# Graph attention on one core: the first four score steps moved in between the value tiles, and the first output tiles' wait lowered by one read

## The reference

```
q = (x @ wq + bq).reshape(N, H, Dh) * Dh ** (-0.5)      # H = 4, Dh = 128
k = (x @ wk + bk).reshape(N, H, Dh)
v = (x @ wv + bv).reshape(N, H, Dh)
scores = jnp.einsum('ehd,ehd->eh', q[src], k[dst])       # one for each edge
... softmax over the edges of each src
out = jax.ops.segment_sum(attn[:, :, None] * v[dst], src, num_segments=N)
return out.reshape(N, D) @ wo + bo
```

## Time and profile before

| | us |
|---|---|
| median of 3 runs | 2468.97 |
| the 3 runs | 2466.75 to 2469.61 |
| the profiled execution, device time | 2466.02 |
| its span in the profile | 2464.0 |
| mean granted TensorE clock | 0.991 |

### The profile page before, as it was taken

The page is one execution under the profiler, slowest core; times in us unless marked ns, Lnnn a source line. Parts: engine busy times, 40 slices in busy tenths (PEclk is TensorE's granted clock), DMA queues, the critical chain, the costliest instruction groups (busy, mean ns, idle before and its releaser), DMA issues. The chain is left out here.

```text
span 2464.0 us, 28010 instructions
## 1 busy us (share of the span) xinstructions
PE 2383.1 (97%) x9352; PEld 1404.5 (57%) x9352; DVE 1428.1 (58%) x2941; ACT 963.0 (39%) x1663; POOL 898.5 (36%) x1246
## 2 busy tenths in 40 slices
PE   8999999999999999999999999999999999998998
PEld 4665655555676646577556567655567664533343
DVE  7896760523775753677564477655377655633345
ACT  5885642221664211566111266321166522211221
POOL 2005202030654430365341165352056443425564
PEclk9999999999999999999999999999999999999999
DMA  5401101320666110366210166410056611679737
GB/s 165 136 18 33 42 13 51 105 88 18 154 154 184 69 59 18 93 156 162 63 42 22 50 163 155 120 44 22 18 133 160 171 42 51 207 236 330 220 91 233
DMA packets 138271, 264.22 MB, mean 107 GB/s; under 512 B 52990, under 2 KB 54766, under 8 KB 135788
## 3 DMA queue, kind: packets, MB, share of 16 engines
q1 hardware_dynamic: 93118, 159.79, 22.3%
q0 software_dynamic: 43664, 100.31, 15.1%
q10 hardware_dynamic: 1346, 2.33, 0.3%
HBM read 212.80 MB, written 31.93 MB: 99 GB/s over the span
## 5 line engine op out<-in xcount | busy, mean ns | idle before, releaser
L114 POOL DMA_DIRECT2D cols<-w x720 | 352.8, 498 | 591.9 <-DVE w L810 576.2
L693 PE MATMUL psum<-cols,rows 128*128 128x256 f32 (+1 forms) x1600 | 370.0, 379 | 7.1 <-DMA cols<-w 7.1
L679 PE MATMUL psum<-g_k_cols,g_q_cols 128*125 128x512 f32 (+1 forms) x960 | 361.4, 513 | 2.5 <-DVE g_row_max L796 2.5
L873 ACT ACTIVATE g_prob<-g_prob,g_row_max 125x1250 f32<-125x1250 f32 x160 | 214.0, 1338 | 306.1 <-DVE g_row_max L796 304.4
L693 PEld LDWEIGHTS psum<-cols,rows 128*128 128x128 f32 (+1 forms) x1600 | 303.4, 190 | 47.0 <-DMA cols<-w 8.5
L796 DVE CUSTOM_DVE_ANT_0 g_prob<-psum,ln_count 125x1250 f32<-125x1250 f32 x160 | 233.6, 1460 | 141.0 <-PE psum L679 141.0
L679 PEld LDWEIGHTS psum<-g_k_cols,g_q_cols 128*125 128x125 f32 x960 | 179.4, 187 | 172.7 <-issue 161.1
L810 DVE STREAM_TRANSPOSE w<-g_prob 128x1280 f32<-128x1280 f32 x160 | 241.2, 1507 | 11.2 <-ACT g_prob L879 11.2
L879 ACT ACTIVATE g_prob<-g_prob,g_row_max 125x1250 f32<-125x1250 f32 x160 | 214.0, 1338 | 58.3 <-DVE g_row_max L786 58.3
L2813 PE MATMUL psum<-m_ew,m_x_cols 128*64 128x256 f32 (+1 forms) x576 | 152.4, 495 | 7.2 <-DMA cols<-in_L_ffn_expert_w,m_weights_of 6.3
L749 PE MATMUL psum<-w,g_k_cols 128*125 128x512 f32 x320 | 150.6, 616 | 0.0
(11 more groups left out here) (393 smaller groups left out, 3967.5 us busy)
## 6 DMA issues: line engine op xcount, KB each, us to landing
cols<-w POOLq DMA_DIRECT2D x720, 80.0 KB, 3.3
cols<-w SPq DMA_DIRECT2D x560, 80.0 KB
m_eb<-in_L_ffn_expert_b SPq DMA_DIRECT2D x54, 192.0 KB
w<-in_L_gnn_m_w SPq DMA_DIRECT2D x8, 1024.0 KB
slot_rows<-p_kf SPq DMA_DIRECT2D x1, 7128.0 KB, 32.7
rows<-slot_rows SPq DMA_DIRECT2D x54, 132.0 KB, 2.9
m_ew<-in_L_ffn_expert_w SPq DMA_DIRECT2D x4, 1536.0 KB, 12.1
slot_outputs<-slot_rows SPq DMA_DIRECT2D x1, 5000.0 KB
```

Source lines behind the costliest of these rows:

```text
L114: return eng.dma_start(out, in_, allow_slow_non_contiguous=True)
L679: ins = pe.matmul(psum[0:P, at:at + width], q_cols[:, h, t * P:(t + 1) * P], k_cols[:, h, start:start + width], start=True, stop=True)
L693: ins = pe.matmul(c.bank(6 + g % 2, 256).rearrange("p (u a i) -> p u a i", u=2, a=SIDE), rows[0:r, j, h * 128:(h + 1) * 128], turned_keys[ ...
L873: s.activation(prob[0:P, u, 0:N], prob[0:P, u, 0:N], ACT.Exp, bias=row_max[:, u, 0:1], scale=-1.0, accum_out=row_max[:, u, 2:3]).then_inc( ...
```

## The change

All of it is in the graph network's layers and holds for each of the four.

- PE's order at a layer's start: values 0 to 3, `scores(0)`, values 4 and 5, `scores(1)`, values 6 and 7, `scores(2)`, value 8, `scores(3)`, value 9, then `scores(4)` and on as before.
- DVE's order follows it: the bias additions, score reads, sums and transposes of the first steps are interleaved in the same way. `turn_squares(2)` still waits for all ten value tiles and now stands ahead of value 9's addition.
- The banks: values 0 to 4 take banks 4, 5, 3, 6, 7, and from there on banks 6 and 7 in turn. Each of the first five waits for the read of the key product that had its bank; value `t` from 5 on waits until value `t-2` is read. `scores(0)` no longer waits for a value to be read, `scores(1)` for three instead of seven or six.
- At the layer's end `outputs(0)` and `outputs(1)` wait for 39 score reads in place of 40, and a wait for the 40th stands ahead of `norm_pe`.

```diff
-    V_BANKS = [0, 2, 4, 5, 3, 1, 6, 7, 6, 7]
-    V_LATE = 7
+    V_BANKS = [4, 5, 3, 6, 7, 6, 7, 6, 7, 6]
+    FIRST_VALUES = [4, 2, 2, 1, 1]
     WEIGH_LAG = 5
...
                 done = 10 * (2 * k_run(l) + 1)
-                if t == 0:
-                    pe.wait_ge(seven_act_made, 8 * (k_run(l) + 1))
...
-                elif t >= 8:
+                if t < 5:
+                    pe.wait_ge(seven_dve_made, done + (1, 2, 9, 7, 8)[t])
+                else:
                     pe.wait_ge(v_made, NT * l + t - 1)
...
                     pe.wait_ge(seven_dve_made, 20 * (k_run(l) + 1))
-                    pe.wait_ge(v_made, NT * l + 6)
                 elif n == 1:
-                    pe.wait_ge(v_made, NT * l + 6)
+                    pe.wait_ge(v_made, NT * l + 3)
...
                 if t < 2:
-                    pe.wait_ge(score_read, STEPS * (l + 1))
+                    pe.wait_ge(score_read, STEPS * (l + 1) - 1)
...
-            for n in range(2, STEPS):
+            for n, count in enumerate(FIRST_VALUES):
+                if n:
+                    scores(n - 1)
+                for t in range(sum(FIRST_VALUES[:n]), sum(FIRST_VALUES[:n]) + count):
+                    values(t)
+            for n in range(len(FIRST_VALUES) - 1, STEPS):
                 scores(n)
                 if n >= WEIGH_LAG:
                     weigh((n - WEIGH_LAG) // 2, (n - WEIGH_LAG) % 2)
...
             weigh(PAIRS - 2, 1)
+            pe.wait_ge(score_read, STEPS * (l + 1))
             norm_pe(2 * l, 0)
...
+            for n, count in enumerate(FIRST_VALUES):
+                if n:
+                    scores(n - 1)
+                if n > 1:
+                    turn_squares(n - 2)
+                for t in range(sum(FIRST_VALUES[:n]), sum(FIRST_VALUES[:n]) + count):
+                    values(t)
+                if n:
+                    invert_sum(n - 1)
+            for n in range(len(FIRST_VALUES) - 1, STEPS):
                 scores(n)
-                if n > 2:
-                    turn_squares(n - 1)
+                turn_squares(n - 1)
                 invert_sum(n)
```

## The result

The changed kernel takes **2483.85 us** (median of 6 runs, 2480.62 to 2490.65) where the kernel before takes 2468.77 us (6 runs): 1.0062 times as long, 95% interval 1.0049 to 1.0076. It is 15.1 us slower, by the medians; the forecast was 14.3 us slower and 2483 us. The profiled execution took 2480.62 us, with a span of 2478.8 us, which is 14.8 us over that of before.

The account below looks back on a forecast made before the run. The prediction took PE, busy for 97% of the span, as the bound. Four layers at 1.5 us of longer stall plus 2.1 us of lowered clock gave +14.3 us, 2483 us against the median; range 2472 to 2488 us.

Parts of the forecast that it names:

- What bounds the kernel, and the layout: PE at each layer's start: PE bounds; last value moves 4.20 us later, no wait ahead of it, scores(5)'s 0.64 us wait goes.
- The moves of pair 0: Ahead of each layer's first weighing: DMAs wait for the last value, flight 8.28 us, PE stalls 4.3 us; +1.5 us per layer.
- The clock: At each layer's first weighing: the new idle stretch lowers PE's clock, costing 2.1 us per layer (0 to 2.8).
- The outputs' wait: At the layer's end: waiting for 39 score reads, then the 40th ahead of norm_pe, costs and brings nothing.
- The sum: Four layers at 1.5 + 2.1 us: +14.3 us, 2483 us against the median of the runs.
- The first: Rival at the first weighings: stall without a fall of the clock, +2 to +7 us, 2471 to 2476 us; chance 0.16.
- The second: Rival at pair 0's DMAs: flight shrinks below its old cover, faster by at most 11 us, 2458 us; chance 0.05.
- The third: Rival: further stalls at pair 1 or values in two banks, 1 to 3 us per layer, 2487 to 2496 us; chance 0.10.
- the fourth: Rival at the first weighing: the change does nothing, weighing at 628.6 without a fall of the clock, 2469 us; chance 0.02.

Follow-up runs that it names:

- experiment 2: Changed kernel with value tiles multiplying k_cols and pair 0's DMAs waiting for the key product alone, not the ten value tiles: 2461.74 us, ratio 0.9968 to the kernel before.
- experiment 1: Changed kernel with five unused matmuls of 512 columns between scores(5) and each layer's first weighing: 2476.28 us, ratio 1.0020 to the kernel before.
- experiment 3: Kernel before with only the outputs' wait changed (39 score reads, the 40th awaited ahead of norm_pe): 2469.48 us, ratio 1.0000.
- experiments 7 and 8: Changed kernel with FIRST_VALUES = [7, 1, 1, 1]: 2468.88 us; changed kernel with two unused matmuls in each layer's idle stretch: 2476.84 us.
- experiment 4: Kernel before, in its own order, with only the new value banks and their waits: 2470.54 us, ratio 1.0004.
- experiments 5 and 6: WEIGH_LAG = 7 in place of 5, layer's end rearranged: on the changed kernel 2463.08 us; on the kernel before, old order and banks, 2469.72 us.

## Why the prediction was right

**What bounds the kernel, and the layout.** Right. The last value was laid out to end 42.7 us behind the first one's start and did (620.36 - 577.63 = 42.73). No value and no score step waits ahead of it, and `scores(5)` no longer waits.

**The moves of pair 0.** Right: the last value is their gate (experiment 2), SP's first DMA stands 42.9 us behind the first value (43.0 forecast). The flight from SP's first DMA to the weighing was taken as 8.28 us; it took 8.44, 8.65, 8.03 and 8.42 us, mean 8.39. The stall of 4.3 us (bounds 3.2 to 4.6) was 4.03 to 4.64 us. The term was +1.5 us for each layer, the measured +1.55. Pair 1 does not wait, as laid out: SP's DMAs of it start 6.2 us behind the last value's end, the forecast distance. The Trainium skill's page DMA: Bandwidth & Descriptors (section on the anatomy of one DMA) gives its fit for a single DMA on the path of those issued by GpSimd (POOL here); the prediction's estimate of 5.0 us stretched it to a batch of 16 from two queues, and for such a batch it does not hold in any of the four layers.

**The clock.** The mechanism was right in all four layers and was the larger half of the loss, as experiment 1 shows by taking it away. The size was under-set: 2.1 us taken, 1.76 to 2.83 measured, mean 2.47, so 9.9 us in place of 8.4. The 2.1 us were taken from the row of the 4.73 us wait, by its eight matmuls alone (5.75 - 3.60 = 2.15 us). The two matmuls of line 454 ahead of them ran at the low clock too and were left out. The rows of before that follow give the same ten records at full clock:

```profile
875.37 0.60 PE L454 MATMUL psum<-cond_w_parts,cond_parts 108*125 108x512 bf16 x2
875.81 3.60 PE L749 MATMUL psum<-w,g_k_cols 128*125 128x512 f32 x8
...
879.24 0.60 PE L454 MATMUL psum<-cond_w_parts,cond_parts 108*125 108x512 bf16 x2
```

That is 879.24 - 875.37 = 3.87 us against 875.37 - 868.91 = 6.46 us, a cost of 2.59 us, which is near the mean measured. The prediction also took the cost to follow from the length of the gap. It followed from where the clock fell: the first layer, where it fell behind the start of the work, has the lowest cost (1.76 us) with a gap of 4.27 us, and the third, where it fell in the idle time, the highest (2.83 us) with the shortest gap, 3.86 us. That idleness lowers the clock and work brings it back, as the Trainium skill says on its page TensorE: Matmul & The Clock Gate (Part 1), agrees with each of these layers.

**The outputs' wait.** Right for this lag: nothing (experiment 3).

**The sum.** 14.3 us forecast, 15.1 by the medians (12 to 19 by the interval), 14.8 between the profiled executions. The trace gives 6.2 us to the stall (5.9 forecast) and 9.9 to the clock (8.4 forecast), 16.1 in all. The profiled executions come as near as they do to the forecast in part by luck: differences outside the changed place, above all the earlier start of the graph network, hide 1.3 us.

**The rivals.** The first (no fall of the clock) was wrong for gaps of 3.9 us and more; experiments 7 and 8 show that it would have been half right for gaps near 2 to 2.6 us. The second (a shorter flight) and the third (a second stall, at pair 1 or in the two banks) did not occur, nor did the fourth (no difference); the two banks were also shown to cost nothing by themselves (experiment 4). What the prediction did not see is that the order it judged as a loss is the better one as soon as the lag is lengthened (experiments 5 and 6).

## What to carry to other kernels

Work that is moved ahead of an event brings nothing if the chain that it feeds is gated by that event; it then only takes away what covered the chain behind the gate. Count what stands between gate and use, and lengthen the lag of the pipeline together with the reorder: here the order alone cost 15 us, the lag alone brought nothing, and both together gained 5.6 us over the kernel before. An idle stretch of the tensor engine should be priced with the clock that it costs: here each of about 4 us cost 1.8 to 2.8 us more than itself.

## What the runs showed of the hardware

- Useless matmuls in an idle stretch made the kernel 10.4 us faster (1.0062 to 1.0020), since PE's clock then never fell there.
- The granted clock fell at all four idle stretches of 3.86 to 4.48 us. It fell behind two of four from 1.78 to 2.25 us (2.25 and 1.94, not 2.13 and 1.78) and behind two of four from 2.40 to 2.64 us (2.64 and 2.59). Length alone does not decide in that range; what does was not tested.
- The clock can fall when work has begun again: at 629 us, within the first microsecond behind an idle stretch of 4.27 us, and so did the four falls of experiments 7 and 8, within 1.5 us of work. In the other three layers of the changed kernel it fell 1.3 to 1.8 us ahead of the work. What a fall costs went with this: 1.76 us in the first case, 2.58 to 2.83 in the second. Two idle stretches of the same 4.73 us, at the same place in two executions, cost 1.71 us (fall behind the start of the work) and 2.59 us (fall ahead of it).
- Sixteen DMAs of 80 KB from SBUF to SBUF, issued by SP and POOL together, took 8.0 to 8.7 us from the first issue until PE went on.
